# Eight bf16 matmuls without a reader ahead of each half of a region's transposes

## The chip, the cores and the metric

The kernel runs on one core of a Trainium2 chip. The metric is the device time of one launch in microseconds (us). Five engines work side by side, each through its own list of instructions in order: TensorE (PE in the profile, with its weight loads apart as PEld), VectorE (DVE), ScalarE (ACT), GpSimd (POOL) and SyncE (SP), which issues the transfers. They meet at semaphores. TensorE writes its results into PSUM banks, from which ScalarE copies them out.

## What is computed

Two layers on an image batch of 8 x 56 x 56 x 64, all in float32. Layer 0 is window attention with routing, followed by a mixture of experts; layer 1 is a convolution with signs as weights, followed by another mixture of experts. The part around the change is the attention: each of the 7 x 7 regions of an image takes the keys and values of its 4 best regions, every one of its 64 tokens keeps the 32 largest of 256 scores per head, and a softmax over these weighs the values.

```python
key_g = ks_[bI, hI, rg]                      # keys of the 4 chosen regions: 256
val_g = vs[bI, hI, rg]
attn = jnp.einsum('bhnsd,bhnkd->bhnsk', qs * scale, key_g.reshape(B, nh, nreg, TS, hd))
score, index = jax.lax.top_k(attn, TS // 8)  # 32 of 256
v_sel = vflat[bI2, hI2, nI2, index]
a_g = jax.nn.softmax(score, axis=-1)
out = jnp.einsum('bhnsk,bhnskd->bhnsd', a_g, v_sel)
```

After it come a 3x3 depthwise convolution of v, an output projection and a residual; then layer norm, router, top 2 of 8 experts and GELU; then the same shape again with the sign convolution and 8 experts of width 128.

## The kernel before

The image batch is 56 strips of 448 tokens (8 rows of 56 pixels), 7 regions each, 392 regions in all. The program is one software pipeline over turns. A turn is two strips, that is 14 slots; in each slot every engine does one region's attention work (stage b) and, at places given by a table of numbers (`PLACES`), a step of the other stages for other strips: a (layer norm, q, k, v), t (choice of the 4 regions), c0 (convolution, projection and experts of layer 0) and c1 (the same of layer 1). The integer part of a place is the slot, the fraction sets where in the slot the step stands. In the steady part of the program 28 turns carry attention.

Stage b of one region, in order:

- TensorE computes the scores (`pe_scores`, L425, tile `s_ps`), two slots ahead. ScalarE copies them into `b_s` (`act_scores`, L435).
- VectorE finds the 32 largest of each row (`dve_select`): four rounds of MAX8 (L452) and MATCH_REPLACE8 (L463) for four column blocks. It waits for the scores and for the probabilities of the region two before, whose buffer `b_r` it reuses. These selections are most of VectorE's work.
- ScalarE takes the maximum and the sum of exponentials (`act_sum`, L475, L478) and the exponentials of all scores (`act_exp`, L485).
- GpSimd inverts the sum (L493), masks (L502) and multiplies into the probabilities `b_e` (L510), which raises `b_prob`.
- TensorE transposes the probabilities in two halves of four 128x128 blocks (`pe_turn`, L524) through one bank, `pT_ps`. ScalarE copies each half out into `b_pT` (`act_turn`, L532), which raises `b_ptc`; the second half can't be written before the first is copied out.
- TensorE multiplies with the values (`pe_values`, L545, bank `o_ps`); ScalarE copies the result into `b_at` (`act_values`, L552), which raises `b_att`.

In slot r TensorE works through: the steps placed below 0.2, the first half of the transposes of region r - 1, the scores of region r + 2, the second half, the steps placed from 0.2 to 0.6, the values of region r - 1, and the steps placed above 0.6. ScalarE's order is: sum and exponentials of region r, the steps below 0.2, the first copy of `pT_ps`, the copies of the scores, the second copy of `pT_ps`, the later steps. GpSimd's is: inverse and mask of region r, the expert steps between 0.2 and 0.5, the probabilities of region r, the rest.

The experts come in the slots of the places 86, 87 (c0) and 110 to 112 (c1): TensorE multiplies with the first weights (L666, banks `h_ps` and `a_ps`) and spreads the gate (L669, `g_ps`), ScalarE applies GELU (L737) and copies the gate (L739, tile `c_cb`), GpSimd multiplies the two (L762), TensorE multiplies with the second weights (L685, `y_ps`). The convolutions are L611, L612 and L616 (c0) and L619, L622 and L623 (c1). `sel_b` and `ident_b` are constant bf16 tables in SBUF. ScalarE loads a new function table where it goes from one of exponential and GELU to the other (ACT_TABLE_LOAD).

Of the kernel before, what the change touches and what calls it, by code (L numbers as in the profile page):

```python
# [41 lines left out]
def program(nc, x, out, w):  # L42
    ctx = ExitStack()
    with ctx:
        def sb(name, shape, dt=F32):
            return ctx.enter_context(nc.sbuf_tensor(name, shape, dt))

        def pb(name):
            return ctx.enter_context(nc.psum_tensor(name, [128, 512], F32))
# [5 lines left out]
        def sem(name, start=0):  # L55
            s = ctx.enter_context(nc.semaphore(name))
            if start:
                ahead.append((s, start))
            return s
# [4 lines left out]
        def alone(eng):  # L64

            eng.sem_inc(passed[eng.engine], 1)
# [32 lines left out]
        ident_b = sb("ident_b", [128, 128], BF16)  # L99
        sel_b = [sb(f"sel_b{n}", [128, g, 128], BF16) for n, g in ((0, NE // 2), (1, NE))]  # L100
# [76 lines left out]
        pT_ps, o_ps, a_ps = pb("pT_ps"), pb("o_ps"), pb("a_ps")  # L177
# [30 lines left out]
        b_ptc = sem("b_ptc", 1)  # L208
        b_pv = sem("b_pv", RING)
        b_att = sem("b_att", 1)  # L210
        cs = []
        for layer in (0, 1):
            n = f"c{layer}_"
# [292 lines left out]
        def pool_prob(pool, tau, r):  # L506
# [3 lines left out]
            pool.tensor_tensor(out=b_e[p][:, :, :], in0=b_e[p][:, :, :], in1=b_r[p][:, :, :],  # L510
                               op=ALU.mult).then_inc(b_prob, 1)

        def pe_turn(pe, tau, r, half):

            reg, p = tau * SLOTS + r, r % 2
            if half == 0:
                pe.wait_ge(b_prob, reg + 3)
                alone(pe)
            pe.wait_ge(b_ptc, 2 * reg + half + 1)
            alone(pe)  # L520
            for t in range(2 * half, 2 * half + 2):
                for c in range(2):
                    col = (t % 2) * 256 + c * 128
                    last = pe.transpose(pT_ps[:, col:col + 128], b_e[p][:, t, c * 128:(c + 1) * 128], k["ident"][:, :])  # L524
            last.then_inc(b_pt, 1)
# [258 lines left out]
        def dve_c(dve, tau, i, step, layer):  # L784
# [77 lines left out]
            if step == 7:  # L862
# [29 lines left out]
            pe={("a", 3): 7.9, ("a", 4): 8.9, ("t", 1): 59.8,  # L892
                ("c0", 0): 78.1, ("c0", TURN): 78.5, ("c0", TURNED): 78.68, ("c0", 2): 81.66, ("c0", GATE): 82.05,
                ("c0", GATED): 82.31, ("c0", 4): 85.64, ("c0", 8): 92.3, ("c0", LOW): 92.55, ("c0", LOWED): 92.69,
                ("c1", 0): 102.1, ("c1", TURN): 102.5, ("c1", TURNED): 102.68, ("c1", 2): 106.695, ("c1", GATE): 107.05,
                ("c1", GATED): 107.31, ("c1", 4): 109.64},
# [135 lines left out]
        with nc.Block() as block:  # L1032
# [21 lines left out]
            @block.tensor  # L1054
            def _(pe):
                fs = dict(a=pe_a, t=pe_t, c=pe_c)

                def turn(n, lo):
                    b, first, last = n - B_TURNS[0], lo == B_TURNS[0], lo == B_TURNS[1] - 1
                    on = B_TURNS[0] <= lo < B_TURNS[1]  # L1060
                    if first:
                        pe_scores(pe, b, 0)
                        pe_scores(pe, b, 1)
                    for r in range(SLOTS):
                        before = on and (r >= 1 or not first)
                        steps(pe, "pe", n, lo, r, fs, 0, 0.2)
                        if before:
                            pe_turn(pe, b, r - 1, 0)
                        if on and (r + 2 < SLOTS or not last):
                            pe_scores(pe, b, r + 2)  # L1070
                        if before:
                            pe_turn(pe, b, r - 1, 1)
                        steps(pe, "pe", n, lo, r, fs, 0.2, 0.4)
                        steps(pe, "pe", n, lo, r, fs, 0.4, 0.6)
                        if before:
                            pe_values(pe, b, r - 1)
                        steps(pe, "pe", n, lo, r, fs, 0.6, 1)
                    if last:
                        pe_turn(pe, b, SLOTS - 1, 0)
                        pe_turn(pe, b, SLOTS - 1, 1)  # L1080
                        pe_values(pe, b, SLOTS - 1)
                run(pe, turn)
# [122 lines left out]
```

## Time and profile before

| | us |
|---|---|
| median of 3 runs | 6430.86 |
| lowest and highest run | 6424.47, 6435.86 |
| the profiled execution | 6440.11 |
| its span from the first to the last instruction | 6438.2 |

The profiled execution is 9.3 us above the median of the runs. Its mean granted TensorE clock is 0.73 of full speed. The times in a row are microseconds from the span's start; "idle before" is what the engine stood still ahead of that row, with what ended the wait. VectorE has the largest busy share, TensorE the next.

### The profile page before, as it was taken

The page shows a single profiled execution, that of the slowest core. Times are in us where ns is not written, and L with a number is a line of the kernel's source. Part 1 is how long each engine was busy: PE and PEld are TensorE (multiplying, and loading weights), DVE is VectorE, ACT ScalarE, POOL GpSimd, SP SyncE. Part 2 cuts the span into 40 slices and gives each one's busy share as a digit, 9 for nine tenths or more (in the row PEclk, how much of TensorE's full clock was granted, in tenths as well). Part 3 has the DMA queues.
Part 4 walks back from the last instruction along what each step waited for, and adds up shares of the span by engine and source line. Part 5 has one row for each costly group of instructions (what it writes and reads, how often), then busy time and mean ns, then how long its engine had stood idle before and what let it go on. Part 6 is the DMA issues. An engine that isn't in the chain of part 4 may idle for free.

```text
span 6438.2 us, 135940 instructions
## 1 busy us (share of the span) xinstructions
PE 4737.3 (74%) x26938; PEld 2880.6 (45%) x26938; DVE 5596.4 (87%) x24453; ACT 4054.4 (63%) x10222; POOL 4425.8 (69%) x3986
## 2 busy tenths in 40 slices
PE   3566777777777777777777777777777777777776
PEld 1333444444444444444444444444444444444444
DVE  1999999988989998999989898989999899999941
ACT  2455666666666666666666666666666666666643
POOL 1667776767677776767677677767776777777742
PEclk9666767777777777777777777777777777777777
DMA  4111111111111111111111111111111111111100
GB/s 75 39 31 42 34 40 34 40 32 42 30 41 34 39 35 34 40 32 43 32 42 30 40 36 36 38 33 40 32 43 31 43 31 32 30 30 34 33 11 10
DMA packets 585501, 229.09 MB, mean 36 GB/s; under 512 B 481152, under 2 KB 580224, under 8 KB 584576
## 3 DMA queue, kind: packets, MB, share of 16 engines
q1 hardware_dynamic: 584576, 219.25, 15.4%
q8 instruction: 276, 4.52, 0.3%
q14 instruction: 649, 5.32, 0.3%
HBM read 150.14 MB, written 68.80 MB: 34 GB/s over the span
## 4 chain that ended last, share of the span: by engine, by line
PE 29%; ACT 18%; issue 16%; DVE 15%; POOL 12%; ACTq 0%; DVEq 0%; POOLq 0%; DMA 0%; SPq 0%
DVE b_v L452 7%; POOL b_r L502 5%; PE y_ps L685 4%; DVE b_r L463 4%; PE h_ps L611 4%; POOL c_h L762 4%; ACT b_x L478 3%; PE a_ps L666 3%; PE pT_ps L524 3%; PE o_ps L545 2%; ACT b_e L485 2%; ACT L737 2%; PE h_ps L666 2%; POOL b_rec L493 2%; ACT L478 2%
## 5 line engine op out<-in xcount | busy, mean ns | idle before, releaser
L463 DVE MATCH_REPLACE8 b_r<-b_v,b_r 128x256 f32<-128x256 f32 x4704 | 1879.1, 416 | 0.0
L502 POOL TENSOR_SCALAR b_r<-b_r,b_rec 128x256 f32<-128x256 f32 x1568 | 1777.1, 1147 | 119.6 <-POOL b_rec L493 119.6
L452 DVE MAX8 b_v<-b_r 128x8 f32<-128x256 f32 x4704 | 1649.2, 418 | 0.0
L524 PE MATMUL pT_ps<-k_ident,b_e 128*128 128x128 f32 x3136 | 669.9, 352 | 776.3 <-ACT b_pT L532 688.3
L493 POOL TENSOR_TENSOR b_rec<-b_den,k_mone 128x4 f32<-128x4 f32 x392 | 400.5, 1022 | 1153.5 <-ACT b_x L478 1150.2
L762 POOL TENSOR_TENSOR c_h<-c_h,c_cb 128x448 f32<-128x448 f32 x672 | 760.9, 1133 | 503.9 <-ACT c_cb L739 503.0
L524 PEld LDWEIGHTS pT_ps<-k_ident,b_e 128*128 128x128 f32 x3136 | 472.6, 180 | 1161.2 <-issue 1136.2
L510 POOL TENSOR_TENSOR b_e<-b_e,b_r 128x1024 f32<-128x1024 f32 x392 | 923.5, 2356 | 18.0 <-POOL b_r L502 14.4
L685 PE MATMUL y_ps<-k_w,c_h 128*112 128x64 f32 x5376 | 776.1, 298 | 181.1 <-POOL c_h L762 177.9
L685 PEld LDWEIGHTS y_ps<-k_w,c_h 128*112 128x112 f32 x5376 | 706.5, 210 | 404.1 <-issue 403.0
L452 DVE MAX8 b_v<-b_s 128x8 f32<-128x256 f32 x1568 | 551.1, 415 | 318.0 <-POOL b_e L510 201.2
L532 ACT ACTIVATE b_pT<-pT_ps 128x512 f32<-128x512 f32 x784 | 469.9, 599 | 432.3 <-PE pT_ps L524 432.0
L485 ACT ACTIVATE b_e<-b_s,b_nm 128x256 f32<-128x256 f32 x1568 | 662.1, 493 | 0.0
L463 DVE MATCH_REPLACE8 b_r<-b_v,b_s 128x256 f32<-128x256 f32 x1568 | 624.7, 413 | 0.0
L666 PE MATMUL h_ps<-c_xT,k_w 128*128 128x448 f32 x672 | 525.4, 879 | 74.0 <-issue 67.5
L425 PE MATMUL s_ps<-b_k,b_q 32*128 32x256 f32 x3136 | 559.5, 484 | 24.2 <-DMA b_q<-q_d 24.2
L435 ACT ACTIVATE b_s<-s_ps 128x512 f32<-128x512 f32 x784 | 427.0, 603 | 117.5 <-PE s_ps L425 117.3
L478 ACT ACTIVATE b_x<-b_v,b_nm 128x32 f32<-128x32 f32 x1568 | 484.2, 310 | 9.5
L666 PE MATMUL a_ps<-c_xT,k_w 128*128 128x448 f32 x672 | 451.5, 765 | 0.0
L425 PEld LDWEIGHTS s_ps<-b_k,b_q 32*128 32x128 f32 x3136 | 336.3, 233 | 155.7 <-issue 119.6
L463 DVE MATCH_VALUE_LOAD b_r<-b_v,b_r 128x8 f32 x4704 | 405.3, 86 | 0.0
L737 ACT ACTIVATE c_h<-h_ps,k_b 128x448 f32<-128x448 f32 x336 | 212.8, 633 | 271.2 <-PE h_ps L666 268.5
(146 smaller groups left out, 7904.9 us busy)
## 6 DMA issues: line engine op xcount, KB each, us to landing
q_d<-a_qe SPq DMA_DIRECT2D x56, 448.0 KB, 4.2
b_k<-k_d SPq DMA_DIRECT2D x1568, 16.0 KB, 2.0
b_v<-v_d SPq DMA_DIRECT2D x1568, 16.0 KB, 2.0
b_q<-q_d SPq DMA_DIRECT2D x392, 64.0 KB, 2.1
c_win<-vpad_d SPq DMA_DIRECT2D x56, 145.0 KB, 2.8
c_hm<-cpad_d SPq DMA_DIRECT2D x56, 145.0 KB, 2.3
vpad_d<-a_vT SPq DMA_DIRECT2D x56, 116.0 KB, 3.7
c_win<-vpad_d SPq DMA_DIRECT2D x56, 116.0 KB, 2.7
```

Of the source, the lines that this page charges most:

```text
L425: last = pe.matmul(s_ps[g][:, t * NKEY:(t + 1) * NKEY], b_q[r % RING][part, 2 * t:2 * t + 2, :].rearrange("c h t -> c (h t)"), b_k[r % RIN ...
L452: top = dve.max(out=b_v8[p][:, t, 8 * rnd:8 * rnd + 8], in_=src[:, t, :])
L463: last = dve.match_replace(out=b_r[p][:, t, :], in_to_replace=b_v8[p][:, t, 8 * rnd:8 * rnd + 8], in_values=src[:, t, :], imm_value=GONE)
L478: last = act.activation(b_x8[:, t, :], b_v8[p][:, t, :], ACT.Exp, bias=b_nm[p][:, t:t + 1], accum_out=b_den[p][:, t:t + 1])
L485: last = act.activation(b_e[p][:, t, :], b_s[p][:, t, :], ACT.Exp, bias=b_nm[p][:, t:t + 1])
L493: pool.tensor_tensor(out=b_rec[p][:, :], in0=b_den[p][:, :], in1=k["mone"][:, 0:HP], op=ALU.pow).then_inc(b_inv, 1)
L502: last = pool.tensor_scalar(out=b_r[p][:, t, :], in0=b_r[p][:, t, :], scalar1=GONE, scalar2=b_rec[p][:, t:t + 1], op0=ALU.is_le, op1=ALU.mult)
L510: pool.tensor_tensor(out=b_e[p][:, :, :], in0=b_e[p][:, :, :], in1=b_r[p][:, :, :], op=ALU.mult).then_inc(b_prob, 1)
L524: last = pe.transpose(pT_ps[:, col:col + 128], b_e[p][:, t, c * 128:(c + 1) * 128], k["ident"][:, :])
L666: pe.matmul(bank[:, 0:STRIP], w1[layer][:, g, :], D["xT"][:, :], start=True, stop=True).then_inc(S["h"], 1)
L685: last = pe.matmul(y_ps[0:TILE, t * C:(t + 1) * C], D["h"][g % 2][:, t * TILE:(t + 1) * TILE], w2[layer][:, g, :], start=False, stop=(g == ...
L762: pool.tensor_tensor(out=D["h"][g % 2][:, :], in0=D["h"][g % 2][:, :], in1=D["cb"][g % 2][:, :], op=ALU.mult).then_inc(S["hc"], 1)
```

## The change

`pe_turn` gets a helper, `pe_keep`, that issues eight bf16 matmuls of 256 columns, with the 128x128 table `ident_b` as weights and a part of `sel_b[1]` as the moving operand. Nobody reads what they write.

- Ahead of the first half, the wait for `b_ptc` (the bank `pT_ps` has been copied out) is now put first, then the eight matmuls write into `pT_ps`, and then TensorE waits for `b_prob` and transposes.
- Ahead of the second half, TensorE waits for `b_att` of the region before (`o_ps` has been copied out), writes eight matmuls into `o_ps`, and then waits for `b_ptc` and transposes. `pe_values` keeps its own wait for `b_att`.

```diff
+        def pe_keep(pe, ps, n):
+
+            for _ in range(n):
+                pe.matmul(ps[:, 0:256], ident_b[:, :], sel_b[1][:, 0:2, :].rearrange("p e c -> p (e c)"), start=True, stop=True)
+
         def pe_turn(pe, tau, r, half):
 
             reg, p = tau * SLOTS + r, r % 2
+            if half == 1:
+                pe.wait_ge(b_att, reg + 1)
+                alone(pe)
+                pe_keep(pe, o_ps, 8)
+            pe.wait_ge(b_ptc, 2 * reg + half + 1)
+            alone(pe)
+            if half == 0:
+                pe_keep(pe, pT_ps, 8)
             if half == 0:
                 pe.wait_ge(b_prob, reg + 3)
                 alone(pe)
-            pe.wait_ge(b_ptc, 2 * reg + half + 1)
-            alone(pe)
```

TensorE's list before, in the slot in which the convolution of layer 0 stands ahead of the transposes (L616 is its last matmul, L692 and L630 are steps of c0 behind them):

```order
L616 MATMUL h_ps<-b_at,k_att 64x448 x2
L524 MATMUL pT_ps<-k_ident,b_e 128x128 x4
L425 MATMUL s_ps<-b_k,b_q 128x256 x4
L524 MATMUL pT_ps<-k_ident,b_e 128x128 x4
L692 MATMUL g_ps<-ident_b,c_x 128x112 x4
L630 MATMUL a_ps<-k_ident,c_yT 112x64 x4
```

The same place in the changed kernel (lines have moved down by 11 from L525 on):

```order
L627 MATMUL h_ps<-b_at,k_att 64x448 x2
L516 MATMUL pT_ps<-sel_b,ident_b 128x256 x8
L535 MATMUL pT_ps<-k_ident,b_e 128x128 x4
L425 MATMUL s_ps<-b_k,b_q 128x256 x4
L516 MATMUL o_ps<-sel_b,ident_b 128x256 x8
L535 MATMUL pT_ps<-k_ident,b_e 128x128 x4
L703 MATMUL g_ps<-ident_b,c_x 128x112 x4
L641 MATMUL a_ps<-k_ident,c_yT 112x64 x4
```

Two blocks of eight matmuls now stand in line, one ahead of the first transposes and so ahead of the scores, one between the scores and the second transposes. Nothing else has moved.

TensorE's list before, one slot later, in the slot of the first two experts of c0:

```order
L666 MATMUL h_ps<-c_xT,k_w_0 128x448
L669 MATMUL g_ps<-c_cwT,sel_b 128x448
L524 MATMUL pT_ps<-k_ident,b_e 128x128 x4
L425 MATMUL s_ps<-b_k,b_q 128x256 x4
L524 MATMUL pT_ps<-k_ident,b_e 128x128 x4
L666 MATMUL a_ps<-c_xT,k_w_0 128x448
```

And in the changed kernel, up to the second block:

```order
L677 MATMUL h_ps<-c_xT,k_w_0 128x448
L680 MATMUL g_ps<-c_cwT,sel_b 128x448
L516 MATMUL pT_ps<-sel_b,ident_b 128x256 x8
L535 MATMUL pT_ps<-k_ident,b_e 128x128 x4
L425 MATMUL s_ps<-b_k,b_q 128x256 x4
L516 MATMUL o_ps<-sel_b,ident_b 128x256 x8
```

The second expert's matmul (L666 into `a_ps`, now L677) stands behind both blocks. The lists of the other engines are unchanged, and so is every slot's pair of blocks: 16 added matmuls for each of 392 regions, 6272 in all, each with its own weight load.

## Rows read from the trace of the kernel before

**Rows 1.** The page, part 1: busy us, share of the span and instructions.

```profile
PE 4737.3 (74%) x26938; PEld 2880.6 (45%) x26938; DVE 5596.4 (87%) x24453; ACT 4054.4 (63%) x10222; POOL 4425.8 (69%) x3986
```

**Rows 2.** Waits of VectorE: waited for, us in total, times, longest.

```profile
DVE b_v L452 <- POOL b_e L510: 201.2, 40, 5.8
...
DVE c_z L834 <- ACT c_p L728: 74.6, 49, 12.6
```

**Rows 3.** Timeline of VectorE: start, duration, instruction, [idle before]. Where it stood still.

```profile
3004.43 1.41 DVE L452 MAX8 b_v<-b_s 128x8 f32<-128x256 f32 x4 [4.84 <-POOL b_e L510]
...
3113.61 1.41 DVE L452 MAX8 b_v<-b_s 128x8 f32<-128x256 f32 x4 [4.88 <-POOL b_e L510]
3126.54 0.19 DVE L834 TENSOR_REDUCE c_z<-c_p 112x4 f32<-112x32 f32 x1 [1.31 <-ACT c_p L728]
```

**Rows 4.** Waits of TensorE ahead of the transposes.

```profile
PE pT_ps L524 <- ACT b_pT L532: 688.3, 210, 7.9
...
PE pT_ps L524 <- POOL b_e L510: 84.7, 63, 4.0
```

**Rows 5.** Timeline of TensorE: nine bf16 matmuls of 448 columns.

```profile
3017.34 1.88 PE L619 MATMUL h_ps<-c_hm,conv_tap 128*64 128x448 bf16 x9 [1.22 <-ACT t_a L381]
```

**Rows 6.** Stretches: length, busy PE, PEld, DVE, ACT, POOL; granted TensorE clock; DMA share.

```profile
3014.00:3024.00 10.00, 7.93 (x59) 4.52 (x58) 8.33 (x47) 6.79 (x21) 9.38 (x9) 0.98 0.13 28
3025.00:3048.00 23.00, 17.80 (x98) 11.45 (x97) 22.68 (x101) 11.49 (x29) 15.45 (x15) 0.50 0.38 77
...
3066.00:3072.00 6.00, 6.00 (x21) 3.41 (x19) 6.00 (x26) 4.67 (x9) 5.70 (x6) 0.50 0.20 45
...
3093.00:3106.00 13.00, 11.40 (x65) 7.39 (x65) 13.00 (x55) 8.48 (x24) 2.96 (x3) 0.50 0.13 35
3107.00:3113.00 6.00, 5.64 (x58) 3.97 (x54) 1.55 (x10) 4.15 (x9) 5.63 (x5) 1.00 0.01 1
```

**Rows 7.** Timelines of TensorE and GpSimd in the slot from 3065 us.

```profile
3066.32 1.06 PE L524 MATMUL pT_ps<-k_ident,b_e 128*128 128x128 f32 x4
3067.31 2.08 PE L425 MATMUL s_ps<-b_k,b_q 32*128 32x256 f32 x8
3069.32 1.12 PE L524 MATMUL pT_ps<-k_ident,b_e 128*128 128x128 f32 x4
3070.22 1.70 PE L666 MATMUL a_ps<-c_xT,k_w 128*128 128x448 f32 x2
...
3073.11 1.14 POOL L762 TENSOR_TENSOR c_h<-c_h,c_cb 128x448 f32<-128x448 f32 x1 [0.79 <-ACT c_cb L739]
```

**Rows 8.** Timelines of TensorE and ScalarE in the slot from 3088 us.

```profile
3089.56 1.13 PE L425 MATMUL s_ps<-b_k,b_q 32*128 32x256 f32 x8
3090.62 0.65 PE L524 MATMUL pT_ps<-k_ident,b_e 128*128 128x128 f32 x4
...
3091.77 0.60 ACT L532 ACTIVATE b_pT<-pT_ps 128x512 f32<-128x512 f32 x1
```

**Rows 9.** Timelines of TensorE, ScalarE and GpSimd in the slot from 3104 us.

```profile
3105.87 1.46 PE L425 MATMUL s_ps<-b_k,b_q 32*128 32x256 f32 x8
3107.26 0.66 PE L524 MATMUL pT_ps<-k_ident,b_e 128*128 128x128 f32 x4
3107.76 0.92 PE L666 MATMUL a_ps<-c_xT,k_w 128*128 128x448 f32 x2
...
3108.89 0.65 ACT L737 ACTIVATE c_h<-a_ps,k_b 128x448 f32<-128x448 f32 x1
...
3110.05 1.13 POOL L762 TENSOR_TENSOR c_h<-c_h,c_cb 128x448 f32<-128x448 f32 x1 [0.37 <-ACT c_cb L739]
3111.14 2.35 POOL L510 TENSOR_TENSOR b_e<-b_e,b_r 128x1024 f32<-128x1024 f32 x1
```

**Rows 10.** Timelines of TensorE and GpSimd in the slot from 3051 us.

```profile
3055.73 1.08 PE L524 MATMUL pT_ps<-k_ident,b_e 128*128 128x128 f32 x4 [3.15 <-ACT b_pT L532]
...
3059.49 1.13 POOL L762 TENSOR_TENSOR c_h<-c_h,c_cb 128x448 f32<-128x448 f32 x1 [1.25 <-ACT c_cb L739]
```

## The prediction

> **What bounds the kernel now.** I read the busy shares first. VectorE is busy for 87% of the span and TensorE for 74% [rows 1]; neither is full, so I went to the waits of VectorE, the fullest engine. Its largest wait is for the probabilities that GpSimd writes, 201.2 us in 40 waits, so 5.0 us each; the next is for an exponential of ScalarE, 74.6 us [rows 2]. The timeline shows where they lie: the long one comes once in a strip, at 3004.43 and at 3113.61, 109.2 us apart [rows 3]. Forty waits are forty strips, that is 20 turns; the other 14 to 16 strips, at the start and the end, have little of it. Between two such waits VectorE works nearly without a break. So the time of a strip is VectorE's work, plus a chain through the other engines that ends in the long wait. Whatever is added to that chain lengthens each of 40 strips; what is added elsewhere is free as long as it stays under VectorE's work.
>
> The chain, followed back from 3113.61: the probabilities (L510, 3111.14), the product of the second expert (L762, 3110.05, after an idle time that ScalarE's copy ended), GELU at 3108.89, and TensorE's L666 at 3107.76 behind the second transposes at 3107.26 [rows 9]. Behind these lies a stretch of 13 us in which TensorE is busy for 11.40 us at a granted clock of 0.50, the lower of its two levels (1.2 GHz) [rows 6]. TensorE is thus on the path for most of the second half of a strip, and half of that at half clock.
>
> **What a block costs.** The nearest rows for bf16 matmuls with a wide moving operand are nine of 448 columns in 1.88 us [rows 5], in a stretch at clock 0.98 [rows 6]. Per column that is 1.88 / 4032 = 0.47 ns, so a block of 8 x 256 = 2048 columns takes 0.95 us at full clock. At half clock, fp32 L666 takes 1.70 us where it takes 0.92 at full [rows 7, 9], 1.85 times as long, so a block takes 1.8 us. All 784 blocks are 745 us of TensorE time at full clock and 1400 at half. The Trainium skill (TensorE: Matmul & The Clock Gate, Back-to-back issue gap) gives N / 2.4 + 2.5 ns for one matmul at full clock. By it a block would be 0.87 us, an estimate, and no row of this case shows this shape; the sum below would fall by about 0.3 us a strip, 12 us in all.
>
> **Where a wait covers it.** TensorE waited 210 times for the first copy ahead of the second transposes, 3.3 us each, and 63 times for GpSimd ahead of the first, 1.3 us each [rows 4]. That is 273 waits at 784 places. At the other 511 TensorE came late and worked on at once, and there a block pushes everything behind it. In a strip of seven slots the second block is covered in three or four (3.15 us of waiting against 0.95 to 1.8 at 3055.73 [rows 10]), and the first in one in part. A first block without a wait of its own is harmless in those slots too, since it only eats into the later wait. Those are the slots of the experts of c1 and the one behind the long wait: cost nothing. The cover would be gone if both blocks ran at half clock there, 3.6 us against 3.15: 0.5 us, hidden by VectorE's work.
>
> **The three slots on the chain**, each with both blocks in line:
>
> - Slot from 3065: TensorE runs from 3066.32 without a gap at clock 0.50 [rows 6, 7], and GpSimd's product at 3073.11 waits 0.79 us for the copy behind L666 and L669. The first block costs 1.8. I expect the clock to be up behind it, since it rose from 0.50 to 1.00 between 3106 and 3107, behind a run of scores and expert matmuls almost without a gap [rows 6], and eight dense matmuls are such work. Then the second block costs 0.95, while scores, transposes and L666 fall from 2.08, 1.12 and 1.70 to 1.13, 0.66 and 0.92 [rows 8, 9]: 2.2 saved. With 0.2 for the gate matmul the slot costs 1.8 + 0.95 - 2.4 = 0.4 us. Without a rise it costs 3.6.
> - Slot from 3088: already at full clock. The first block puts 0.95 in front of transposes and scores, for which ScalarE waits. The second transposes end at 3091.27, 0.5 us before ScalarE comes for them at 3091.77 [rows 8], so the second block costs 0.95 - 0.5 = 0.45. That makes 1.4. The blocks fill the short gap behind which the clock now falls for 13 us [rows 6]; I expect one or two of the next small steps at full clock, 0.6 back. Net 0.8.
> - Slot from 3104: the first block 0.95, minus 0.7 because the transposes and the first scores (1.46 at 3105.87 against 1.13 [rows 8, 9]) now run wholly at full clock; the second block 0.95 in full, since GELU at 3108.89 follows with no idle time. Net 1.2.
>
> Sum on the chain: 0.4 + 0.8 + 1.2 = 2.4 us a strip.
>
> **What comes back.** The exponential for which VectorE waits 1.31 us at 3126.54 [rows 3] hangs on a slot whose second transposes run at half clock (as at 3055.73, 1.08 us [rows 10], against 0.66 [rows 9]); a second block right behind the scores should hold the clock up until then: 0.45. In the slots of c1, 23 us at clock 0.50 [rows 6], the blocks should lift the clock for parts of it, and GpSimd's wait of 1.25 us at 3059.49 [rows 10] is time that this returns to the chain, if it does. Bounds are 0 and 2.5 us (two such waits a strip); I take 1.0, as I expect the lift in one of the two. A loss is excluded here, as each block lies in a wait longer than itself.
>
> Net 2.4 - 0.45 - 1.0 = 0.95 us a strip. Forty strips give 38 us. The other strips, where VectorE hardly waits, lose their cover only in part: 7 us for all. That is 45 us on the profiled 6440, so 6485. The runs shown lie 9 us below the profiled execution, so I forecast **6476 us** as a median, 0.7% slower.
>
> **Rivals.**
>
> 1. *Clock lifted for the chain* (faster). If the blocks hold the clock up in both c1 slots and behind the slot of 3088, the returns are 0.45 + 2.5 + up to 1.0 more from the 11.40 us of half clock work, against 2.4 us: 1.5 us a strip less, 40 x 1.5 = 60, so 6371 us. For it: 11.40 us of path work at half clock is much to win from. Against it: much of that stretch is small steps that alternate with ScalarE, without any block among them, and the blocks come ahead of it. The Trainium skill (TensorE: Matmul & The Clock Gate, Part 1) says "the default state is throttled, and activity releases the throttle". By that rule added matmuls are gain wherever they fill a wait. This case's rows agree on one point only, that the clock is low behind gaps, and show that TensorE at 6.00 of 6 us busy in 3066 to 3072 can still be at 0.50.
> 2. *No lift* (much slower). The blocks stay at half clock in the slots of 3065 and 3104: 3.6 + 1.4 + 2.6 = 7.6 at the worst, and 4.5 if one of them lifts. 40 x 4.5 = 180, so 6610 us. It decides from the point where the clock is not up by the scores of the slot of 3065.
> 3. *A wash*. Costs and returns cancel within 0.3 us a strip, 6418 to 6444 us. For it: both are 2 to 3 us, from the same few rows.
> 4. *It doesn't do what it says*: the blocks don't lie in waits at 511 of 784 places. This is part of the forecast. The waits for `b_ptc` and `b_att` that now come earlier are for copies of the slot before and add nothing.
>
> **How the numbers follow.** The forecast case (6440 to 6540) has 0.42, no lift 0.18, the wash 0.17, the lifted chain 0.23. About 0.2% is what a measurement of this kernel can tell from no change. So faster 0.23, same 0.17, slower 0.60. The range of 6385 to 6600 leaves out some 0.1 of the lifted case and 0.1 of the case without a lift.
>
> **What would show it.** Right: VectorE's wait for `b_e` grows from 5.0 us to 6 or 7; the granted clock rises from 0.73 to 0.78 or more; the waits of TensorE for `b_pT` shrink by most of the block time at their places; VectorE's wait for `c_p` falls. The prediction is wrong if VectorE's long wait shrinks, or if the stretch behind the slot of 3088 runs at full clock, or if the blocks are far from 0.95 us each.

## The result and the profile after

The changed kernel takes 6290.4 us in the median of 4 runs (6287.8 to 6296.4), against 6433.4 for the kernel before in the same comparison: a ratio of 0.9776, 95% interval 0.9755 to 0.9797. It is 2.2% faster, and 0.7% slower was forecast. The profiled execution has a span of 6289.9 us, 148.3 less than before, and a mean granted clock of 0.877 where it was 0.730.

The page of the changed kernel, part 1 (busy time, share, instructions), answers to [rows 1]:

```profile
PE 4771.4 (76%) x33210; PEld 3053.4 (49%) x33210; DVE 5552.6 (88%) x24453; ACT 4050.5 (64%) x10222; POOL 4433.1 (70%) x3986
```

TensorE has 6272 matmuls more and is busy for only 34 us more. The blocks themselves take 903 us (L516, next fence but one), so the old work shrank by some 870 us of busy time: it runs at the higher clock.

VectorE's waits (waited for, us, times, longest), against [rows 2]:

```profile
DVE b_v L452 <- POOL b_e L510: 137.0, 40, 7.5
...
DVE c_z L845 <- ACT c_p L739: 63.4, 41, 11.3
```

The long wait is still there 40 times, but 3.4 us long in place of 5.0. The two entries give back 64 and 11 us. Groups of the changed kernel (busy us, mean ns, idle before), the first two being the added blocks:

```profile
L516 PE MATMUL pT_ps<-sel_b,ident_b 128*128 128x256 bf16 x3136 | 474.8, 302 | 7.0 <-ACT a_qe L344 3.0 <-ACT t_a L381 2.1 <-ACT a_vT L351 1.7
L516 PE MATMUL o_ps<-sel_b,ident_b 128*128 128x256 bf16 x3136 | 428.3, 282 | 0.0
```

The stretches that answer to [rows 6], in the same columns: the one behind the convolution slot, and the slot of the first experts of layer 0.

```profile
3017.00:3030.00 13.00, 10.05 (x98) 7.24 (x96) 13.00 (x53) 10.62 (x29) 4.00 (x4) 1.00 0.09 22
3027.00:3036.00 9.00, 8.06 (x81) 6.14 (x80) 8.00 (x34) 7.13 (x16) 8.56 (x8) 1.00 0.18 47
```

Thirteen microseconds that stood at 0.50 now stand at 1.00.

**One strip, part by part.** Timelines of VectorE and TensorE: the long wait at the strip's start, the convolution's first matmuls, the first block of the slot behind, the transposes behind it, and the long wait at the end.

```profile
2934.25 1.41 DVE L452 MAX8 b_v<-b_s 128x8 f32<-128x256 f32 x4 [3.14 <-POOL b_e L510]
...
3007.04 3.92 PE L622 MATMUL h_ps<-c_win,lepe_tap 128*64 128x448 f32 x6 [3.12 <-ACT a_qe L344]
...
3027.10 1.04 PE L516 MATMUL pT_ps<-sel_b,ident_b 128*128 128x256 bf16 x8
3027.97 0.60 PE L535 MATMUL pT_ps<-k_ident,b_e 128*128 128x128 f32 x4
...
3037.29 1.40 DVE L452 MAX8 b_v<-b_s 128x8 f32<-128x256 f32 x4 [1.76 <-POOL b_e L510]
```

And the same two places of the kernel before:

```profile
3080.58 4.71 PE L611 MATMUL h_ps<-c_win,lepe_tap 128*64 128x448 f32 x6 [3.12 <-ACT a_qe L344]
...
3104.88 1.06 PE L524 MATMUL pT_ps<-k_ident,b_e 128*128 128x128 f32 x4
```

| from, to | before | after | |
|---|---|---|---|
| long wait to convolution (slots of c1 and that of 3065) | 3004.43 to 3080.58: 76.15 | 2934.25 to 3007.04: 72.79 | -3.4 |
| convolution to the next expert slot (slot of 3088 and the 13 us) | to 3104.88: 24.30 | to 3027.10: 20.06 | -4.2 |
| expert slot to long wait (slot of 3104) | to 3113.61: 8.73 | to 3037.29: 10.19 | +1.5 |
| the strip | 109.2 | 103.0 | -6.1 |

The strip is a typical one: over the sixteen turns in the middle of the program (regions 84 to 307) the three parts of this strip went from 76.6, 23.5 and 8.9 us to 72.8, 20.2 and 10.2 in the mean. So the slot of 3104 costs about what was forecast, and the two stretches ahead of it give far more back than was forecast.

The other strip of each turn gains little: in the mean 80.1, 23.8 and 8.7 us became 80.6, 21.2 and 10.2, together 0.6 us less. TensorE's list has the end of its loop in it, and there it stood still for over 3 us ahead of an expert matmul before and after; the clock was low behind that, so the first block ran at half clock (kernel before, then two rows of the changed one):

```profile
3179.50 1.83 PE L666 MATMUL h_ps<-c_xT,k_w 128*128 128x448 f32 x2 [4.55 <-issue]
```

```profile
3099.68 1.83 PE L677 MATMUL h_ps<-c_xT,k_w 128*128 128x448 f32 x2 [3.49 <-issue]
...
3101.68 1.91 PE L516 MATMUL pT_ps<-sel_b,ident_b 128*128 128x256 bf16 x8
3103.39 1.06 PE L535 MATMUL pT_ps<-k_ident,b_e 128*128 128x128 f32 x4
```

That block pushes the transposes by 1.7 us. A pair of strips went from 221.9 us (3126.54 minus 2904.65, the same instruction a turn apart) to about 215 us. Between the first transposes of region 56 and those of region 336, twenty turns apart, lie 4407.7 us before and 4285.2 after, so 122 of the 148 us; another 15 are gained ahead of them and 11 behind.

### The profile page after: what moved, and what is told of

Its sections match the earlier page's. It is cut to its first block and busy times, and to the rows that moved or that the text cites. A ratio compares the mean times of both kernels' runs of the same rounds, so it can differ in the third digit from the quotient of the medians.

```text
span 6289.9 us, 148876 instructions
## 1 busy us (share of the span) xinstructions
PE 4771.4 (76%) x33210; PEld 3053.4 (49%) x33210; DVE 5552.6 (88%) x24453; ACT 4050.5 (64%) x10222; POOL 4433.1 (70%) x3986
## 5 line engine op out<-in xcount | busy, mean ns | idle before, releaser
L502 POOL TENSOR_SCALAR b_r<-b_r,b_rec 128x256 f32<-128x256 f32 x1568 | 1777.3, 1147 | 119.6 <-POOL b_rec L493 119.6
L696 PE MATMUL y_ps<-k_w,c_h 128*112 128x64 f32 x5376 | 724.3, 283 | 296.5 <-POOL c_h L773 294.5
L510 POOL TENSOR_TENSOR b_e<-b_e,b_r 128x1024 f32<-128x1024 f32 x392 | 927.2, 2365 | 18.0 <-POOL b_r L502 14.4
L535 PE MATMUL pT_ps<-k_ident,b_e 128*128 128x128 f32 x3136 | 530.2, 296 | 516.4 <-ACT b_pT L543 483.3
L696 PEld LDWEIGHTS y_ps<-k_w,c_h 128*112 128x112 f32 x5376 | 647.8, 195 | 488.3 <-issue 487.7
L535 PEld LDWEIGHTS pT_ps<-k_ident,b_e 128*128 128x128 f32 x3136 | 395.7, 154 | 596.0 <-issue 585.9
L463 DVE MATCH_VALUE_LOAD b_r<-b_v,b_r 128x8 f32 x4704 | 526.1, 112 | 0.0
L425 PE MATMUL s_ps<-b_k,b_q 32*128 32x256 f32 x3136 | 469.8, 419 | 24.2 <-DMA b_q<-q_d 24.2
L516 PE MATMUL pT_ps<-sel_b,ident_b 128*128 128x256 bf16 x3136 | 474.8, 302 | 7.0 <-ACT a_qe L344 3.0
L677 PE MATMUL h_ps<-c_xT,k_w 128*128 128x448 f32 x672 | 394.3, 674 | 72.8 <-issue 66.3
L516 PEld LDWEIGHTS pT_ps<-sel_b,ident_b 128*128 128x128 bf16 x3136 | 329.5, 108 | 244.2 <-issue 175.3
L516 PE MATMUL o_ps<-sel_b,ident_b 128*128 128x256 bf16 x3136 | 428.3, 282 | 0.0
```

The source lines that it names most:

```text
L425: last = pe.matmul(s_ps[g][:, t * NKEY:(t + 1) * NKEY], b_q[r % RING][part, 2 * t:2 * t + 2, :].rearrange("c h t -> c (h t)"), b_k[r % RIN ...
L463: last = dve.match_replace(out=b_r[p][:, t, :], in_to_replace=b_v8[p][:, t, 8 * rnd:8 * rnd + 8], in_values=src[:, t, :], imm_value=GONE)
L502: last = pool.tensor_scalar(out=b_r[p][:, t, :], in0=b_r[p][:, t, :], scalar1=GONE, scalar2=b_rec[p][:, t:t + 1], op0=ALU.is_le, op1=ALU.mult)
L516: pe.matmul(ps[:, 0:256], ident_b[:, :], sel_b[1][:, 0:2, :].rearrange("p e c -> p (e c)"), start=True, stop=True)
L696: last = pe.matmul(y_ps[0:TILE, t * C:(t + 1) * C], D["h"][g % 2][:, t * TILE:(t + 1) * TILE], w2[layer][:, g, :], start=False, stop=(g == ...
```

## The experiments

All times are medians; ratios are to the kernel before, run beside them. A slot is named by its number in the strip, as r modulo 7 of the slot in which the transposes stand: 1 is the convolution slot of layer 0 (3088), 2 its first experts (3104), 3 the slot behind VectorE's long wait, 4 the convolution of layer 1, 5 and 6 the slots of its experts with a long wait for ScalarE (second halves at 3039 and 3055), 0 that of its last experts (3065). In every one of these kernels the attention is computed in full; only the matmuls without a reader differ.

**The waits alone.** The theory: the gain is the clock. The rival: it is the order of the waits.

```diff
             if half == 1:
                 pe.wait_ge(b_att, reg + 1)
                 alone(pe)
-                pe_keep(pe, o_ps, 8)
+                pass
...
             if half == 0:
-                pe_keep(pe, pT_ps, 8)
+                pass
```

> The changed kernel without the 6272 matmuls: the waits stand in their new order, nothing is added. Theory C (the gain comes from the granted clock that the blocks hold up, above all in the 13 us behind the transposes of the convolution slot of layer 0): no gain without blocks, 6420 to 6445 us, mean clock 0.73. Rival W (part of the gain comes from the new order of the waits): 6300 to 6400 us.

6425.0 us, ratio 0.9992 (0.9981 to 1.0003), clock 0.741. The order of the waits is worth nothing; what follows is due to the matmuls.

**One block of the two.** e2 drops the second call of `pe_keep`, e3 the first.

> Only the block ahead of the first half of the transposes. Theory C: the first block alone makes TensorE busy for one stretch, but the gap behind the scores stays; about half of the gain, 6340 to 6390 us, mean clock 0.79 to 0.83. Rival F (the first block does it all, the second only costs): 6260 to 6290 us.

6379.2 us, ratio 0.9902 (0.9864 to 0.9939), clock 0.796.

> Only the block between the scores and the second half. Theory C: it lies right at the gap behind which the clock fell, so it gives more than the first block, 6290 to 6350 us, mean clock 0.80 to 0.85. Rival F: little or no gain, 6400 to 6440 us.

6295.4 us, ratio 0.9808 (0.9770 to 0.9846), clock 0.847. The block between scores and second half does nearly all, with half the matmuls. Adding the first block, which lies ahead of the scores and mostly in no wait, raises the mean clock to 0.877 and leaves the time where it was within the intervals.

**Where the gain lies.** The calls were tied to slots:

```diff
-                pe_keep(pe, o_ps, 8)
+                if (r + 1) % NWIN in (1,):
+                    pe_keep(pe, o_ps, 8)
```

and the same for the first block. I took the convolution slot first, since 11.40 us of half clock work stood behind it [rows 6].

> Both blocks, but only in the one slot of seven in which the convolution of layer 0 stands ahead of the transposes: 896 matmuls in place of 6272. Theory C: 2 to 3 us a strip come back from the 13 us stretch behind it, so 6310 to 6350 us, mean clock about 0.78. Rival E (the gain comes from the slots of the experts of layer 1, where the blocks lie in waits): 6410 to 6440 us.

6449.0 us, ratio 1.0024 (1.0011 to 1.0037), clock 0.762. Theory C falls in the form in which I had put it: this slot alone brings nothing, it costs a little (more than rival E had allowed for). Its timelines (TensorE's convolution, the transposes of the next slot, VectorE's long wait) show why:

```profile
3079.64 4.71 PE L624 MATMUL h_ps<-c_win,lepe_tap 128*64 128x448 f32 x6 [3.21 <-ACT a_qe L344]
...
3100.84 0.60 PE L537 MATMUL pT_ps<-k_ident,b_e 128*128 128x128 f32 x4
...
3104.89 0.63 PE L537 MATMUL pT_ps<-k_ident,b_e 128*128 128x128 f32 x4 [2.39 <-ACT b_pT L545]
...
3111.50 1.41 DVE L452 MAX8 b_v<-b_s 128x8 f32<-128x256 f32 x4 [3.99 <-POOL b_e L510]
```

From convolution to the next slot TensorE takes 21.2 us in place of 24.3, blocks included. But then it waits 2.39 us for ScalarE ahead of the second half, where the kernel before had no wait. Of 3.1 us, 1.2 reach VectorE (31.9 us from convolution to long wait, 33.0 before). In the other strip of that turn (convolution at 2970.36, long wait ended at 3003.74) none do: 33.4 us. Over the same sixteen turns as above, the way from convolution to long wait went from 32.4 to 32.1 us in the one strip and from 32.5 to 33.2 in the other.

The kernel before has the same lesson in it. In three of the 32 strips of these turns its own stretch behind the convolution slot ran at a granted clock of 0.87 to 1.00 without any added matmul. At 2206 us it did, and the transposes of the next slot came 11.6 us behind those of the convolution slot (2202.53 to 2214.15), where they mostly come 15.9 behind:

```profile
2206.00:2213.00 7.00, 4.72 (x55) 3.29 (x56) 7.00 (x30) 4.92 (x15) 0.03 (x1) 1.00 0.04 8
```

The turn around it is only 1 us shorter than most. So a fast stretch there is not by itself a fast turn.

Then the complement, and the three slots of layer 1's experts:

> Both blocks in six of seven slots, none in the convolution slot of layer 0. The run with blocks in that slot alone gave no gain (ratio 1.0024). Theory L (the gain comes from the slots of the experts of layer 1 and the slot before the convolution, where TensorE reaches the convolution earlier): all of the gain or more, 6270 to 6310 us. Rival J (neither place is enough, the stretch behind the convolution slot pays only when the rest is at full clock as well): half of the gain, 6330 to 6390 us.

6295.3 us, ratio 0.9779 (0.9761 to 0.9798), clock 0.843: all of the gain, without the convolution slot. In the strip that gains, the way from convolution to the next expert slot takes 20.0 us in the mean of the sixteen turns, as short as in the changed kernel (20.2), though no block stands in it; in the other strip it is 24.0, as before.

> Both blocks only in the three slots of the experts of layer 1 (two with a wait ahead of the second half, the third without). Theory L: two thirds or more of the gain, 6290 to 6340 us. Rival J: 6370 to 6420 us.

6333.6 us, ratio 0.9852 (0.9827 to 0.9878), clock 0.805. Three of seven slots carry two thirds of the gain. Theory L holds. Here too the stretch behind the convolution slot can be fast without a block in it; in six strips of the 32 it runs wholly at full clock:

```profile
3682.00:3689.00 7.00, 4.58 (x54) 3.19 (x55) 7.00 (x29) 4.99 (x16) 0.20 (x1) 1.00 0.03 7
```

The slots 3 and 4 were not tested by themselves.

> Both blocks only in the slot of the first two experts of layer 0, where the forecast had them in full on the chain (first 0.95 us minus 0.7, second 0.95). Theory P (a block without a wait costs what it lasts, and nothing behind this slot gives it back): 0.5 to 1.9 us a strip, 6450 to 6500 us. Rival G (in this slot too the clock gives the time back): 6400 to 6440 us.

6429.7 us, ratio 0.9991 (0.9978 to 1.0004). By its time this falls to rival G. The blocks cost 1.2 to 1.6 us on the way from this slot to the long wait, in the mean of the sixteen turns. They are given back elsewhere: in one strip ahead of the convolution (80.1 us became 77.8), in the other behind it (23.5 became 21.3, with 1.1 us lost ahead of it). The mean clock is 0.766.

**Which blocks of those slots.** Second blocks only, in the two slots with long waits, where by the words of the change they should be free:

> Only the second block, and only in the two slots of layer 1's experts in which TensorE waits over 3 us for ScalarE's copy ahead of the second half: 1792 matmuls, each block shorter than its wait. Theory L (these waits are where added work is free and the lifted clock pays): 6340 to 6400 us, a good part of the 1.5 to 2% of the run with three slots. Rival S (it takes the blocks outside the waits to lift the clock): 6415 to 6440 us.

6431.4 us, ratio 0.9990 (0.9976 to 1.0004), clock 0.735: nothing. The time is that of rival S; its reason is not borne out by e15 below, where blocks in these waits alone do bring a gain. At this point it was open whether slot 0 carries the gain, or both blocks in 5 and 6, or the blocks in the waits were too short.

> Both blocks, only in the two slots of layer 1's experts with a long wait. Theory B (first and second block together make TensorE dense enough that the second half and the expert matmuls behind the wait run at full clock): 6340 to 6380 us, clock 1.0 at the second halves there. Rival Z (the third slot carries the gain): 6415 to 6440 us.

6358.4 us, ratio 0.9878 (0.9862 to 0.9895), clock 0.781. Theory B holds: 1.2% from 5 and 6 alone.

> Both blocks, only in the third slot of layer 1's experts, ahead of the q and k matmuls; no wait there. Theory B: 6420 to 6450 us, since the blocks cost what they give. Rival Z: 6330 to 6380 us.

6412.9 us, ratio 0.9957 (0.9940 to 0.9974), a little better than theory B had it and far from rival Z. Slot 0, which I had put at +0.4 us a strip, gives 0.4%. With the 1.2% this makes about the 1.5% of the three.

> Only second blocks in the two slots with long waits, but 32 and 20 matmuls long, so that the waits are nearly full. If eight were too few to hold the clock: 6330 to 6390 us. If that clock is worth nothing to the chain: 6415 to 6440 us. At half clock 32 matmuls last 7 us, longer than the wait; then it is slower, up to 6500 us.

6374.2 us, ratio 0.9895 (0.9875 to 0.9915), clock 0.779. The edit:

```diff
-                pe_keep(pe, o_ps, 8)
+                pe_keep(pe, o_ps, {5: 32, 6: 20}.get((r + 1) % NWIN, 0))
```

TensorE's waits for the first copy and VectorE's long waits (us, times, longest), in the run with eight and in the run with 32 and 20:

```profile
PE pT_ps L536 <- ACT b_pT L544: 554.1, 207, 7.0
...
DVE b_v L452 <- POOL b_e L510: 201.1, 41, 5.8
```

```profile
PE pT_ps L535 <- ACT b_pT L543: 351.4, 157, 4.5
...
DVE b_v L452 <- POOL b_e L510: 173.3, 40, 6.0
```

Eight matmuls left 2.0 to 3.2 us of each of these waits idle in the mean, the mean clock stayed at 0.735, and VectorE waited as before [rows 2]. With the waits filled or nearly so, the work behind them runs at a granted clock of 0.84 to 0.95 in the mean, and VectorE waits 28 us less. So filling these waits is worth 1%, and the short block alone in them is worth nothing. How the time comes back is seen in GpSimd's waits for ScalarE's copy of the gate, which follows TensorE's expert matmuls; kernel before, changed kernel, and the run with both blocks in 5 and 6:

```profile
POOL c_h L762 <- ACT c_cb L739: 503.0, 325, 20.6
```

```profile
POOL c_h L773 <- ACT c_cb L750: 342.1, 172, 20.7
```

```profile
POOL c_h L775 <- ACT c_cb L752: 390.3, 238, 21.7
```

The wait of 1.25 us at 3059.49 [rows 10] is gone at the same place of the changed kernel, where the two products follow one another, and 161 us of GpSimd's waits with it.

```profile
2980.28 4.52 POOL L502 TENSOR_SCALAR b_r<-b_r,b_rec 128x256 f32<-128x256 f32 x4 [0.30 <-POOL b_rec L493]
2984.77 2.33 POOL L773 TENSOR_TENSOR c_h<-c_h,c_cb 128x448 f32<-128x448 f32 x2
2987.05 2.37 POOL L510 TENSOR_TENSOR b_e<-b_e,b_r 128x1024 f32<-128x1024 f32 x1
```

**What kind of work.** The block's matmul was replaced by an fp32 transpose of `k["ident"]`:

```diff
-                pe.matmul(ps[:, 0:256], ident_b[:, :], sel_b[1][:, 0:2, :].rearrange("p e c -> p (e c)"), start=True, stop=True)
+                pe.transpose(ps[:, 0:128], k["ident"][:, :], k["ident"][:, :])
```

> The same places, but each block is eight fp32 transposes of 128 columns in place of eight bf16 matmuls of 256; they take about 1.1 us at full clock by the four of a half at 0.60. Theory A (whatever keeps TensorE in work lifts the clock): 6290 to 6330 us, mean clock 0.86. Rival K (transposes don't hold the clock up as matmuls do): the blocks only cost, 6450 to 6600 us, mean clock 0.75 or less.

6299.2 us, ratio 0.9785 (0.9767 to 0.9803), clock 0.877. Theory A: transposes do it as well.

**Filling more waits.** Before the convolution of layer 0 TensorE stood still for 3.12 us. A block there, into the bank that the convolution is about to overwrite, and no first blocks:

```diff
+                if 12:
+                    pe_keep(pe, h_ps, 12)
                 pe.wait_ge(a_ev, 5 * s + 13)
                 alone(pe)
```

> Only the second block, in all slots, and a further block of 12 matmuls into h_ps in the wait for the copies of q and k ahead of the convolution of layer 0, where TensorE stood still for 3.1 us and the clock had fallen by the first of the convolution's matmuls. Theory C (the clock of the work on the chain is what counts): the convolution runs at full clock throughout and 1 us a strip comes back, 6230 to 6270 us. Rival: that the convolution isn't on the chain once the rest is faster, 6290 to 6310 us.

6213.2 us, ratio 0.9646 (0.9623 to 0.9668), clock 0.846. More than I expected. The convolution's matmuls (mean ns), changed kernel and this one:

```profile
L622 PE MATMUL h_ps<-c_win,lepe_tap 128*64 128x448 f32 x336 | 224.4, 830 | 146.0 <-ACT a_qe L344 146.0
```

```profile
L624 PE MATMUL h_ps<-c_win,lepe_tap 128*64 128x448 f32 x336 | 145.6, 571 | 78.0 <-ACT a_qe L346 78.0
```

The twelve matmuls don't fill the wait: 1.7 us of its 3.1 stay idle (78.0 us in 46 waits). VectorE's long wait has mostly gone, to 37.1 us in 14 waits:

```profile
DVE b_v L454 <- POOL b_e L512: 37.1, 14, 4.9
```

Against the second block alone (6295) this is 82 us for 672 matmuls, 1.5 us a strip.

> As the run with the second block and the block in the convolution's wait (6213 us), but 16 matmuls in the second block of the three slots with a wait of 3 us or more. Theory C (the clock fell because a block of 0.9 us leaves most of such a wait idle): 6150 to 6200 us, mean clock 0.88 or more. Rival D (VectorE is the bound by now and the clock buys nothing more): 6205 to 6220 us.

6189.9 us, ratio 0.9618 (0.9595 to 0.9642), clock 0.879: in the range of theory C, though less for the clock gained than the steps before.

> As that run too, but without the second block in the slot of the first two experts of layer 0, where it lies on the chain. Theory P: 0.5 to 0.9 us a strip come back, 6175 to 6200 us, if VectorE still waits there; rival D: 6205 to 6220 us.

6226.6 us, ratio 0.9663 (0.9634 to 0.9692). Neither theory: taking the uncovered block away makes it no faster, and its interval overlaps that of the run with it.

> As the run at 6190 us, but with the waits nearly full: 28, 32 and 20 matmuls in the three long waits, 16 in the convolution's. Theory C: 6150 to 6185 us, mean clock above 0.90. Rival D (VectorE is the bound): 6180 to 6200 us. A block that outlasts its wait at half clock would make it slower, 6200 to 6260 us.

6184.8 us, ratio 0.9606 (0.9585 to 0.9627), clock 0.889. The same as the run at 6190 within the intervals, and the clock is short of the 0.90 of theory C. VectorE is busy for 91% of the span in both, which speaks for rival D. Both beat the changed kernel by 1.6 to 1.7% and the kernel before by 3.8 to 3.9%.

## Why the prediction was wrong

The step that failed is the price of the returned clock: 0.6 us a strip behind the slot of 3088 and 1.0 us in the c1 slots. Per turn of two strips, and leaving the exponential aside, the forecast had -1.2 us ahead of the convolution (twice 0.4 - 1.0), +1.6 from there to the slot of 3104 and +2.4 behind it. In the mean of the sixteen turns these parts measured -3.3, -5.9 and +2.9. Both signs that the prediction had named for being wrong came: VectorE's long wait shrank, and the stretch behind the slot of 3088 ran at full clock.

- **What bounds the kernel**: right. The chain into VectorE's long wait sets the time, and the gain came through it. One thing was missed: I took 40 strips as alike, though the loop's end falls into every second one, and there the part with the c1 slots gives nothing back (80.1 us before, 80.6 after).
- **The block's price**, 0.95 us at full clock and 1.8 at half: right. The rows show 0.87 (3027.10 to 3027.97) and 1.71 (3101.68 to 3103.39). The estimate from the Trainium skill (TensorE: Matmul & The Clock Gate, Back-to-back issue gap), 0.87 us, agrees with the first.
- **Slot of 3065, +0.4**: the number came out in the first strip, by luck. From its first block to the next step's matmul L257 the changed kernel takes 9.22 us (2992.45 to 3001.67), the one before 8.88 (3066.32 to 3075.20). But the first block didn't cost the 1.8 us of half clock: the clock was already up, and it took 0.87. In its place came waits that the sum didn't have, such as 0.74 us for ScalarE's copy ahead of the second half. Blocks there alone nonetheless bring 0.4% (e14). A stretch of that slot and TensorE's row behind it:

```profile
2990.00:2996.00 6.00, 5.32 (x39) 3.82 (x39) 6.00 (x27) 5.93 (x19) 5.15 (x7) 1.00 0.09 19
...
2996.71 0.63 PE L535 MATMUL pT_ps<-k_ident,b_e 128*128 128x128 f32 x4 [0.74 <-ACT b_pT L543]
```

- **Slot of 3104, +1.2**: about right, +1.5, of which 0.53 is a wait for ScalarE's copy ahead of the second half (at 3031.14) that the sum didn't have.
- **Slot of 3088, +0.8**: this term failed, and by the most. Convolution, blocks and the 13 us behind them took 4.2 us less. I let the clock rise for "one or two of the next small steps"; it stayed at 1.00 for all thirteen, with TensorE busy for 10.05 of 13 us. Part of it (4.71 to 3.92 us) is the convolution itself, which has no block ahead of it. But the blocks of that slot aren't what turns the sign: alone they cost 0.2% (e4), and without them the gain is the same (e5). The stretch was fast without them too, in e5 and in some strips of e7 and of the kernel before. I had tied its clock to the blocks next to it.
- **Returns in the c1 slots, 1.0 with an upper bound of 2.5**: this term failed too, and blocks there are enough to turn the sign. They were 3.4 us in the strip shown, with the cost of the slot of 3065 in it, so about 3.7; e7, e13 and e14 show that blocks in these slots by themselves make the kernel faster. Part of what they bring lies behind the convolution and not in these slots: in e7 that part went from 23.5 us to 20.3 in the one strip. The bound was worked out from two waits of GpSimd (1.25 us) as the only way back. VectorE's own busy time shrank as well, by 44 us (below). The reason given also failed in part: I had the return from blocks "in a wait longer than itself". Second blocks in the two long waits alone gave nothing (e10). With the first block beside them (e13), or with the waits filled (e15), or with second blocks in all the other slots as well (e3), the time fell. Why these bring the stretches behind them to full clock and the two short blocks don't, the runs leave open.
- **The exponential for which VectorE waits, 0.45 a strip**: right in sign, 11 us in all where 18 were expected.
- **Rivals.** Rival 1, the lifted chain, is what happened, and stronger: 143 us, not 60. The rule of the Trainium skill named there (TensorE: Matmul & The Clock Gate, Part 1), activity releases the throttle, has the mean clock of nearly every run on its side; but a higher mean clock was not always a gain, as e4 (0.762, slower) and e9 (0.766, no change) show. What it would not have told is e10: blocks of eight in the two long waits of layer 1 left the mean clock at 0.735 and the time unchanged. I had weighed the clock by single rows of before at 0.50 with TensorE busy, and gave too little to many small steps that each get faster.

The accounting of the span, 148 us: VectorE's waits for GpSimd 64, for ScalarE's exponential 11, the waits ahead of MAX8 listed under "issue" 18 (93.0 to 74.9 us), less busy time 44, the rest in small waits. The 44 us are no steady return of the clock: in e8, which is faster by another 77 us, VectorE is busy for 5626.8 us, 30 more than in the kernel before.

## What to carry to other kernels

Where TensorE is on the path only for part of the time and its mean granted clock is 0.73, ask what its clock would be worth before counting what filler matmuls cost: price the small dependent steps behind each gap at the other clock level, since they add up. Where filler pays was not to be read off the length of the wait here: 12 matmuls in a 3.1 us wait ahead of a convolution gave 1.3%, eight in each of two waits of 3 to 7 us gave nothing, and 32 and 20 in the same two gave 1%. Test each place alone and all but it: here single slots gave between -0.2 and 0.4%, a pair 1.2%, and all together 2.2%.

Don't add up the gains of single places either. Many turns of these kernels last one of a few times: about 221.8 us in 13 of twenty turns before and in 13 of e14's, 215.0 in 13 of the changed kernel's, 211.6 in ten of e11's (from convolution to convolution). What holds a turn at such a length no run here shows.

## What the runs showed of the hardware

VectorE's two-input subtraction (L247, 112x256, both inputs in SBUF) takes 0.41 us or up to 2.4 us. In the kernel before it met GpSimd's product, and ended 0.28 us behind it, at 3076.83 against 3076.55 (3074.20 + 2.35):

```profile
3074.20 2.35 POOL L510 TENSOR_TENSOR b_e<-b_e,b_r 128x1024 f32<-128x1024 f32 x1
...
3074.60 2.23 DVE L247 TENSOR_TENSOR c_xn<-c_tok,c_mv 112x256 f32<-112x256 f32 x1
```

In the changed kernel GpSimd is earlier relative to it, and the two ends lie 0.29 us apart again:

```profile
3000.36 2.36 POOL L510 TENSOR_TENSOR b_e<-b_e,b_r 128x1024 f32<-128x1024 f32 x1
...
3002.41 0.60 DVE L247 TENSOR_TENSOR c_xn<-c_tok,c_mv 112x256 f32<-112x256 f32 x1
```

Over all 112 of these the busy time fell from 122.5 to 72.4 us. That of the multiplication behind it (L251), which met the same products more often now, rose from 60.2 to 77.9, so the two lines give 32 us of VectorE's 44. In the kernel before all 46 subtractions that began during a product of GpSimd (L510 or L762) ended 0.28 or 0.29 us behind it. But 51 others began during GpSimd's masking (L502, which reads `b_r` in SBUF) and took 0.41 to 0.43 us, as if alone:

```profile
2907.25 4.69 POOL L502 TENSOR_SCALAR b_r<-b_r,b_rec 128x256 f32<-128x256 f32 x4 [0.30 <-POOL b_rec L493]
...
2908.82 0.41 DVE L247 TENSOR_TENSOR c_xn<-c_tok,c_mv 112x256 f32<-112x256 f32 x1
```

The Trainium skill (SBUF — State Buffer, Who interferes with whom) says that a VectorE instruction with two SBUF inputs contends with a GpSimd instruction that reads SBUF. The rows agree for GpSimd's instructions with two wide inputs, and not for the masking with one; the measurement decides.

Added transposes raise the mean clock as added matmuls do. The Trainium skill (TensorE: Matmul & The Clock Gate, Part 4) says that the full clock doesn't engage for transposes. The run with 6272 added fp32 transposes of 128 columns had a mean clock of 0.877, the same as with bf16 matmuls of 256 columns, and 2.0 to 2.3% less time than before. The measurement decides for these fp32 transposes, which stand among the kernel's other matmuls; bf16 ones were not tried.

What stays open: why the cost of the blocks in slot 2 is given back elsewhere when they stand alone (e9), why the stretch behind the convolution slot is at full clock in some strips without a block near it, what holds a turn at one of a few lengths, and by what share VectorE's shorter work, rather than its shorter waits, is owed to each slot.
